# Routing of seven sequences moved into the attention ahead of the experts, with joined moves in the layers beside it

## The chip, the cores and the metric

One core of one Trainium2 chip runs the whole kernel. The metric is the time of one execution on the device in microseconds (us). Of three runs of the kernel before, the median was 2061.19 us (2058.47 to 2065.32).

## What is computed

`x` holds 8 sequences of 128 tokens with 256 columns, `ctx` a context of the same shape. Four layers follow, each a cross attention and a feed-forward network with a residual:

```
x = x + L0_xattn(ln(x), ctx, ctx);  x = x + L0_ffn(ln(x))     # 8 experts, top 2
x = x + L1_xattn(ln(x), ctx, ctx);  x = x + L1_ffn(ln(x))     # ternary weights
x = x + L2_xattn(ln(x), ctx);       x = x + L2_ffn(ln(x))     # attention, then 16 experts
x = x + L3_xattn(ln(x), ctx);       x = x + L3_ffn(ln(x))     # gated, rounded weights
```

The parts that matter here. The L1 feed-forward takes ternary weights from the mean of |w| of each matrix, and quantises rows of activations:

```
ternary(w) = round(tanh(w / (mean|w| + 1e-8))) * arctanh(mean|w|)
linear(x, w, g) = quantise(g * x * rsqrt(mean(x*x) + 1e-8)) @ ternary(w).T
L1_ffn = linear(silu(linear(x, w1, g1)) * linear(x, w2, g2), w3, g3)
```

The L2 feed-forward is a causal self attention with 16 heads of 128, then a layer of experts:

```
hid = h + attention(rmsnorm(h))
x2 = rmsnorm(hid);  probs = softmax(x2 @ gate.T)          # 16 experts
top_w, top_i = top_k(probs, 4);  top_w /= sum(top_w)
routed = sum over the 4 of top_w * w2[e](silu(w1g[e] x2) * (w1u[e] x2))
out = hid + routed + shared(x2)                           # a shared network of width 352
```

## The kernel before, in words

The stages run one after the other, each in blocks in which every engine has its own program and waits on semaphores. SyncE (SP) issues most DMAs, GpSimd (POOL) the indirect ones.

**L1 attention** (`stage_l1_xattn`, L850; from about 397 to 515 us). POOL clears `vs` (L889), builds the parity column (L905), raises the variances to the power -1/2 (L256), makes the masked keys (L913) and normalises probabilities (L921). ScalarE first copies the values into `vs` (L987), then works through 32 steps `n`, four exponentials each (L996). TensorE waits for the copies at its first step.

**L1 feed-forward** (`stage_l1_ffn`, L1058; 515.7 to 671 us). SP loads three weight matrices of 128x2048 and three gains (L1131 to L1135). VectorE normalises x (`normalise_all`, L233 and L238), waits for all loads, sums |w| of the three matrices (L1161), takes thresholds, makes the ternary weights (L1173, L1174), waits for the root mean squares, and then quantises the input of each sequence (`first`, L1187 to L1204). A step for a sequence is `gate` (L1209), `add` of the sequence before (L1234), `first` of a later pair, and `quantise_hidden` (L1215 to L1229). The last begins with the mean square `vh`, which POOL raises to a power (`rh`, L1151). In this stage VectorE also prepares some weights of the next one (L2401).

**L2 attention** (`attention_16`, L1989, causal, prefix `l2fa`; about 1178 to 1521 us). It runs 8 sequences `b` of 4 quads `i`; a quad is 4 heads. The orders are written out by hand. TensorE, for a quad: values of the quad before (L1417), side work of the even half-slot, projections of sequence b+1 (q, k, v: L2279, L2286), output projection of the quad before (L2316), side work of the odd half-slot, transposes of the probabilities (L1409), scores of the next quad (L1401). VectorE, for a quad: maximum (L1366), addition of the output (L2197), copy of the turned output (L2193), normalising the probabilities (L1374, L1376), side work of the even half-slot, copy of v (L2187), side work of the odd half-slot. ScalarE has the exponentials (L1385) and the copies. Half-slot h is 2*(4b+i) for the even and one more for the odd.

The side work of before is `GatedWeightsPrep` (L1445): it prepares the weights of the L3 feed-forward in the half-slots by a fixed table in `on_vector`. For j=0 from half-slot 11 and j=1 from 25: three mask steps (k = 0 to 2), one that inverts (k = 3), three that round (k = 4 to 6, L1542 to L1548), a diagonal (k = 7), two rows (k = 10, 11). The down weights take half-slots 40 to 48, two masks of 704 columns at 40 and 41 and two roundings at 43 and 44.

**Experts** (`moe_16`, L3003; 1522.5 to 1765 us). First comes the whole routing: mean squares on ScalarE, power on POOL (L3136), rows `x2` on VectorE (L3159), transposes, logits (L3340), softmax, comparison of every pair of the 16 scores, choice of four, count of earlier tokens of each expert (a matmul), slot and weight of every choice. POOL scatters each row to its four slots in `rows` in DRAM (32 indirect DMAs, L3148). From it comes the list of tiles (L3229 to L3249): 47 tiles of 128 rows, each with its expert's number. TensorE works on 63 units: first 16 halves of the shared network (two for each sequence), then the 47 tiles. For each unit: up (L3361), transposes of the activation (L3374, L3375), down (L3392, L3393). SP loads the expert weights (L3104 is the last of them), each tile's tokens (L3110), and stores the results.

**L3 attention** (`attention_16` not causal, prefix `l3a`, with the gated feed-forward as side work; 1765.5 to 2064 us). POOL gathers four routed rows for each token of a sequence (L2091). For sequences 0 and 1 VectorE adds them with their weights to x (L2146, four operations each), for later ones POOL does (`mix`, L2099 and on). POOL gathers sequences 0 and 1 first, then raises the variance (L2110) between other work. L1814 is one VectorE operation of the side work there.

Of the kernel before, what the change touches and what calls it, by code (L numbers as in the profile page):

```python
# [13 lines left out]
ALU = mybir.AluOpType  # L14
# [7 lines left out]
P = 128  # L22
B = 8
D = 256
KC = D // P
STAGES = range(5)
# [823 lines left out]
def stage_l1_xattn(nc, G, A):  # L850

    with ExitStack() as ctx:
# [33 lines left out]
        with nc.Block() as block:  # L886
            @block.gpsimd
            def _(pool):
                nc.gpsimd.memset(vs[:, :, :, :, :], 0.0).then_inc(zeroed, 1)  # L889
# [36 lines left out]
                keys(1)  # L926
                for n in range(N):
# [55 lines left out]
            def _(act):  # L983
                act.wait_ge(zeroed, 1)
                for s in range(2):
                    heads = lambda t: t.rearrange("p c b (g s k) -> p (c b) g s k", s=2, k=HD)[:, :, :, s, :]
                    nc.scalar.copy(heads(vs[:, s, :, :, :]), heads(G.ctxT[:, :, :, :])).then_inc(vs_made, 1)  # L987

                for n in range(N):
                    u = n % 2  # L990
                    wait(act, turned, 2 * (n - 1))
# [10 lines left out]
            def _(pe):  # L1002
# [38 lines left out]
                for n in range(N + 3):  # L1041
                    if n + 1 < N:
                        scores(n + 1)
                    if n == 0:
                        pe.wait_ge(vs_made, 2)
# [7 lines left out]
H1 = 1024  # L1053
# [4 lines left out]
def stage_l1_ffn(nc, G, A, W):  # L1058
# [5 lines left out]
    with ExitStack() as ctx:  # L1064
# [5 lines left out]
        w = [T.sb(f"w{j}", [P, NW]) for j in range(3)]  # L1070
        below = T.sb("below", [P, NW], BF16)
        tern = [T.sb(f"tern{j}", [P, NW], BF16) for j in range(3)]
        g12 = T.sb("g12", [P, 2, D])
        g3 = T.sb("g3", [P, H1])
        asum = T.sb("asum", [P, 3])
# [37 lines left out]
        order, first_order, second_order, loaded, summed, totals = (  # L1113
            T.sem("order"), T.sem("first_order"), T.sem("second_order"), T.sem("loaded"), T.sem("summed"), T.sem("totals"))
# [12 lines left out]
        with nc.Block() as block:  # L1127
            @block.sync
            def _(sp):
                for j, (name, chunks) in enumerate((("L1_w1T", KC), ("L1_w2T", KC), ("L1_w3T", HC))):  # L1130
                    sp.dma_start(w[j][:, :].rearrange("p (c o) -> p c o", c=chunks),  # L1131
                                 A[name].rearrange("(c p) o -> p c o", p=P)).then_inc(loaded, 16)
                sp.dma_start(g12[:, 0, :], row(A["L1_ffn_g1"], D)).then_inc(loaded, 16)
                sp.dma_start(g12[:, 1, :], row(A["L1_ffn_g2"], D)).then_inc(loaded, 16)
                sp.dma_start(g3[:, :], row(A["L1_ffn_g3"], H1)).then_inc(loaded, 16)  # L1135
                sp.wait_ge(loaded, 96)
                W.load(sp, A)
# [17 lines left out]
            def _(dve):  # L1155
                T.order = o = Order(dve, order)
                normalise_all(nc, G, T, xn)

                dve.wait_ge(loaded, 96)
                for j in range(3):  # L1160
                    last = nc.vector.tensor_reduce(asum[:, j:j + 1], w[j][:, :], AX.X, ALU.add,  # L1161
                                                   apply_absolute_value=True)
                last.then_inc(summed, 1)
# [8 lines left out]
                for j in range(3):  # L1172
# [4 lines left out]
                    dve.wait_ge(tern_ready, j + 1)  # L1177
                dve.wait_ge(atanh_ready, 1)
                o.step(nc.vector.tensor_scalar(atanh[:, :], atanh[:, :], 0.5, None, ALU.mult))
                dve.wait_ge(squared, 1)  # L1180
                nc.vector.tensor_scalar(vrms[:, :], ss[:, :], 1.0 / D, eps, ALU.mult, ALU.add).then_inc(ms_ready, 1)
                dve.wait_ge(rrms_ready, 1)
# [29 lines left out]
                def quantise_hidden(b, u):  # L1212
# [3 lines left out]
                        .then_inc(vh_ready, 1)  # L1216
                    dve.wait_ge(rh_ready, b + 1)
# [34 lines left out]
            def _(act):  # L1252
                act.wait_ge(T.ln_ready, 1)
# [2281 lines left out]
```

## Time and profile before

| what | value |
|---|---|
| median of three runs | 2061.19 us |
| the profiled execution | 2066.01 us |
| its span | 2064.2 us |
| TensorE (PE) busy | 1600.0 us, 78% |
| VectorE (DVE) busy | 1376.3 us, 67% |
| ScalarE (ACT) busy | 815.3 us, 39% |
| GpSimd (POOL) busy | 627.3 us, 30% |
| mean granted TensorE clock | 0.889 |

The times of stages and instructions below count from the start of the span of the profiled execution. Busy shares are means over stages with different limits, so they are to be read stage by stage. PEld is TensorE's loading of weights, which runs beside its matmuls. PEclk is the granted clock of TensorE as a share of 2.4 GHz: 1.00 is 2.4, 0.50 is 1.2 GHz. "[2.58 <-PE l2fa_psS L1401]" behind a row says that the engine had been idle for 2.58 us before it and that TensorE's work of line 1401 released it. "x4" behind a row merges four instructions that follow each other closely.

### The profile page before, as it was taken

How to read it: one execution, taken by the hardware profiler on the slowest of the kernel's cores; microseconds unless marked ns; L12 is line 12 of the kernel's file. 1: busy time of each engine (PE TensorE's matmuls, PEld its weight loads, DVE VectorE, ACT ScalarE, POOL GpSimd, SP SyncE). 2: the span in 40 equal slices, each digit the busy share in tenths (PEclk: the TensorE clock that was granted, in tenths of full speed). 3: DMA queues.
4: the chain of work that ended last, by engine and by line, in shares of the span. 5: the costliest groups of instructions: out<-in, count | busy, mean ns of one | idle time of the engine just before them, and what ended most of it. 6: DMA issues, size and time to landing. Idle time of an engine off the chain costs nothing. (4 is left out here: it accounts for less than half of the span.)

```text
span 2064.2 us, 29673 instructions
## 1 busy us (share of the span) xinstructions
PE 1600.0 (78%) x9237; PEld 1129.0 (55%) x9318; DVE 1376.3 (67%) x3775; ACT 815.3 (39%) x2357; POOL 627.3 (30%) x744
## 2 busy tenths in 40 slices
PE   3559998698144589888889589999958799498884
PEld 2424443365022366666666468888854455397872
DVE  6679969578676588887888725565347333258776
ACT  2113444355222366666667423333321122144551
POOL 0020002266200587777677430000015100533100
PEclk7579999879555799999999889999979899799996
DMA  1306520000580910000000140000043222622110
GB/s 61 107 1 174 183 81 1 1 1 1 85 151 0 342 64 1 1 1 1 1 1 1 44 151 1 15 1 1 1 167 89 72 89 89 224 103 75 65 47 11
DMA packets 104405, 129.33 MB, mean 63 GB/s; under 512 B 14208, under 2 KB 89184, under 8 KB 101056
## 3 DMA queue, kind: packets, MB, share of 16 engines
q1 hardware_dynamic: 95264, 112.39, 16.9%
q0 software_dynamic: 8992, 15.08, 3.5%
q8 instruction: 78, 1.28, 0.3%
q14 instruction: 71, 0.58, 0.1%
HBM read 85.75 MB, written 46.94 MB: 64 GB/s over the span
## 5 line engine op out<-in xcount | busy, mean ns | idle before, releaser
L580 POOL TENSOR_TENSOR l0f_diag<-g_identb,l0f_mask 128x1024 bf16<-128x1024 bf16 x16 | 32.0, 2026 | 227.7 <-PE l0f_psA L836 208.8
L2769 ACT ACTIVATE l2x_probs<-l2x_psS,l2x_nmax 128x128 f32<-128x128 f32 x256 | 91.0, 373 | 10.6 <-DVE l2x_nmax L2683 10.5
L2553 POOL TENSOR_TENSOR l2x_probs<-l2x_probs,l2x_rtotal 128x512 f32<-128x512 f32 x64 | 66.9, 1045 | 91.2 <-DVE l2x_rtotal L2689 91.2
L3129 POOL MEMSET moe_before<- 128x256 f32 x1 | 0.3, 317 | 287.2 <-POOLq L162 287.2
L3260 DVE COPY moe_xgT<-moe_psX 128x256 f32<-128x256 f32 x47 | 20.0, 425 | 99.7 <-PE moe_psX L3368 99.7
L2564 POOL TENSOR_TENSOR l2x_vsm<-l2x_vraw,l2x_smooth_row 128x512 f32<-128x512 f32 x64 | 84.7, 1344 | 3.9 <-ACT l2x_vraw L2803 3.6
L2091 POOL DMA_INDIRECT l3a_routed<-rows,slots_slot_of x32 | 31.5, 984 | 174.0 <-issue 165.8
L2914 PEld LDWEIGHTS l2x_psS<-l2x_kT,l2x_qT 128*128 128x128 f32 x512 | 66.8, 191 | 22.3 <-issue 17.9
L996 ACT ACTIVATE l1a_probs<-l1a_psS,l1a_nmax 128x256 f32<-128x256 f32 x128 | 59.0, 473 | 43.7 <-PE l1a_psT L1024 36.9
L819 PE MATMUL l0f_psH<-l0f_wT,l0f_xm 128*128 128x512 bf16 x256 | 68.0, 389 | 10.2 <-DVE l0f_h L660 9.0
L921 POOL TENSOR_TENSOR l1a_probs<-l1a_probs,l1a_rtotal 128x512 f32<-128x512 f32 x64 | 65.2, 1041 | 32.5 <-DVE l1a_rtotal L958 32.5
L3361 PE MATMUL moe_psG<-moe_w,moe_xgT 128*128 x188 | 69.2, 491 | 5.0 <-issue 1.6
L2812 ACT COPY l2x_pT<-l2x_psT 128x512 f32<-128x512 f32 x64 | 37.5, 586 | 89.6 <-PE l2x_psT L2922 89.6
L2316 PE MATMUL l3a_psY<-l3a_wo,l3a_oT 128*128 128x256 f32 x256 | 61.6, 383 | 12.4 <-DVE l3a_oT L2193 12.3
L1385 ACT ACTIVATE l2fa_probs<-l2fa_psS,l2fa_bias 128x128 f32<-128x128 f32 x128 | 45.3, 366 | 63.2 <-DVE l2fa_bias L1369 63.2
L2930 PE MATMUL l2x_psO<-l2x_pT,l2x_vsm 128*128 128x128 f32 x512 | 69.8, 281 | 0.0
L2914 PE MATMUL l2x_psS<-l2x_kT,l2x_qT 128*128 128x128 f32 x512 | 67.8, 275 | 1.8 <-ACT l2x_probs L2769 1.7
L2187 DVE COPY l2fa_v<-l2fa_psQ 128x512 f32<-128x512 f32 x32 | 22.0, 688 | 70.0 <-PE l2fa_psQ L2286 65.3
L2279 PE MATMUL l3a_psQ<-l3a_xT,l3a_wq 128*128 128x128 f32 x512 | 65.1, 282 | 2.9 <-ACT l3a_qT L2238 1.5
L2535 POOL TENSOR_TENSOR l2x_qrstd<-l2x_qve,g_minus_half 128x4 f32<-128x4 f32 x64 | 65.7, 1026 | 5.3
L3313 ACT ACTIVATE moe_gated<-moe_psG 128x176 f32<-128x176 f32 x63 | 20.0, 318 | 119.7 <-PE moe_psG L3361 111.7
L2786 ACT ACTIVATE l2x_qT<-l2x_psN,cw_head_bs,cw_head_ws 128x512 f32<-128x512 f32 x64 | 50.3, 786 | 41.4 <-PE l2x_psN L2865 41.4
(543 smaller groups left out, 4870.3 us busy)
## 6 DMA issues: line engine op xcount, KB each, us to landing
rows<-l2x_zero SPq DMA_DIRECT2D x1, 18304.0 KB, 59.9
kT_ctx<-l0f_held SPq DMA_DIRECT2D x32, 256.0 KB, 3.6
v_ctx<-l0f_held SPq DMA_DIRECT2D x32, 256.0 KB, 3.7
l3a_kT<-kT_ctx SPq DMA_DIRECT2D x8, 1024.0 KB, 6.6
l3a_v<-v_ctx SPq DMA_DIRECT2D x8, 1024.0 KB, 5.1
l0f_wrow<-in_L_ffn_w SPq DMA_DIRECT2D x24, 256.0 KB, 3.1
moe_xg<-rows SPq DMA_DIRECT2D x47, 128.0 KB, 2.0
rows<-moe_yg SPq DMA_DIRECT2D x47, 128.0 KB, 1.7
```

Of the source, the lines that this page charges most:

```text
L819: last = nc.tensor.matmul(psH[:, k, :], xm[b % 2][:, k, c, e, :], wT[:, 2 * e:2 * e + 2, c, :], start=(e == 0 and c == 0), stop=(e == E0 - ...
L921: nc.gpsimd.tensor_tensor(probs[:, u, j, :, :], probs[:, u, j, :, :], rtotal[:, u, j, :].unsqueeze(2).to_broadcast([P, 2, D]), ALU.mult)\
L996: last = nc.scalar.activation(probs[:, u, j, m, :], psS[2 * u + j][:, m, :], ACT.Exp, bias=nmax[:, u, j, m:m + 1], scale=1.0, accum_out=to ...
L2279: last = nc.tensor.matmul(psQ[bank][:, j, :], w[:, c, h * HD:(h + 1) * HD], xT[u][:, c, :], start=(c == 0), stop=(c == KC - 1))
L2316: last = nc.tensor.matmul(psY[:, :], oT[:, i % 2, j, :], wo[:, 4 * i + j, :], start=(i == 0 and j == 0), stop=(i == QUADS - 1 and j == 3))
L2535: ins = nc.gpsimd.tensor_tensor(qrstd[:, t % 2, :], qve[:, :], G.minus_half[:, 0:4], ALU.pow)
L2553: nc.gpsimd.tensor_tensor(probs[:, n % 2, :, :], probs[:, n % 2, :, :], rtotal[:, n % 2, :].unsqueeze(2).to_broadcast([P, 4, P]), ALU.mult)\
L2564: nc.gpsimd.tensor_tensor(vsm[:, j % 3, 4 * g:4 * g + 4, :].rearrange("p (g r) d -> p g r d", r=2), vraw[:, j % 2, 2 * g:2 * g + 2, :].uns ...
L2769: last = nc.scalar.activation(probs[:, n % 2, j, :], psS[:, j, :], ACT.Exp, bias=nmax[:, n % 2, j:j + 1], scale=1.0, accum_out=total[:, n ...
L2914: last = nc.tensor.matmul(psS[:, j, :], qT[:, n % 4, j, :], kT[:, n // 2 % 2, 2 * (n % 2) + j // 2, :], start=True, stop=True)
L2930: last = nc.tensor.matmul(psO[:, j, :], vsm[:, n // 2 % 3, 4 * (n % 2) + j, :], pT[:, n % 2, j, :], start=True, stop=True)
L3361: last = nc.tensor.matmul(psG[m % 3][:, 0:2 * I2], x, w, start=(c == 0), stop=(c == KC - 1))
```

## The change

**L1.** A new class `TernaryWeights` loads the three matrices and the gains during the L1 attention, and ScalarE sums |w| there, with an activation Abs over 2048 columns at steps 8, 12 and 16. The clearing of `vs` goes behind the first two groups of keys on POOL, the copies into `vs` to ScalarE's step 1, the wait of TensorE to step 3. In the L1 feed-forward the wait for the loads and the three reductions are gone; the order on VectorE is: statistics, thresholds, ternary matrix 0, normalised x, ternary matrix 1, mean squares, ternary matrix 2, first. The logarithm goes ahead of the squares on ScalarE. The add of the sequence before goes from behind the gate to behind `vh`.

```diff
+class TernaryWeights:
+    SUMS_AT = (8, 12, 16)
...
+    def sum(self, nc, act, n):
+        if n in self.SUMS_AT:
+            j = self.SUMS_AT.index(n)
+            act.wait_ge(self.loaded[j], 16)
+            wait(act, self.summed, j)
+            nc.scalar.activation(self.magnitude[:, :], self.w[j][:, :], ACT.Abs, accum_out=self.asum[:, j:j + 1])\
+                .then_inc(self.summed, 1)
...
                     nc.vector.tensor_scalar(vh[:, u:u + 1], hh[:, u:u + 1], 1.0 / H1, eps, ALU.mult, ALU.add)\
                         .then_inc(vh_ready, 1)
+                    if not is_zero(b):
+                        add(b - 1, 1 - u)
                     dve.wait_ge(rh_ready, b + 1)
...
                     gate(b, u)
-                    if not is_zero(b):
-                        add(b - 1, 1 - u)
```

**L2, routing.** A new class `Router` does the routing for one sequence at a time. Sequences 0 to 6 are routed in half-slots of the causal attention, beside `GatedWeightsPrep` (class `PrepAndRoutes`; in a half-slot the preparation comes first). For sequence s, with t = TURN_AT[s]: ScalarE's square and VectorE's variance in half-slot t-2, the rows `x2` in t-1, TensorE's transposes and VectorE's copy in t, logits, maximum and exponential in t+1, comparison in t+2, choice and TensorE's count in t+3, slots and weights in t+4. POOL has, in this order for each s: power, addition of hid to x, four scatters. All routings share one bank of PSUM with the preparation. The slots and weights of sequence 6 are made behind the last quad, its scatter and all of sequence 7 in the MoE stage.

```diff
+class Router:
+    TURN_AT = (12, 23, 28, 37, 49, 54, 60)
...
+    def compare(self, dve, s):
+        nc, o = self.nc, self.o
+        dve.wait_ge(self.exp_ready, s + 1)
+        o.step(nc.vector.reciprocal(self.total[:, :], self.total[:, :]))
+        o.step(nc.vector.tensor_scalar(self.scores, self.scores, self.total[:, :], None, ALU.mult))
+        full = [P, E2, E2]
+        other, own = self.scores.unsqueeze(1).to_broadcast(full), self.scores.unsqueeze(2).to_broadcast(full)
+        o.mark(nc.vector.tensor_tensor(self.gt, other, own, ALU.is_gt))
+        o.step(nc.vector.tensor_tensor(self.eq, other, own, ALU.is_equal))
+        o.step(nc.vector.tensor_tensor(self.eq, self.eq, self.before[:, :, :], ALU.mult))
+        o.step(nc.vector.tensor_tensor(self.gt, self.gt, self.eq, ALU.add))
+
+    def choose(self, dve, s):
+        nc, o = self.nc, self.o
+        o.step(nc.vector.tensor_reduce(self.rank, self.gt, AX.X, ALU.add))
+        o.step(nc.vector.tensor_scalar(self.chosen[:, :], self.rank, TOP2 - 0.5, None, ALU.is_lt))
+        old, new = self.earlier[:, s % 2, :], self.earlier[:, (s + 1) % 2, :]
...
+            ins = nc.vector.tensor_tensor(new, old, self.chosen[:, :], ALU.add)
+        ins.then_inc(self.chosen_ready, 1)
+        full = [P, TOP2, E2]
+        o.step(nc.vector.tensor_tensor(self.is_kth, self.rank.unsqueeze(1).to_broadcast(full),
+                                       self.numbers[:, 0:TOP2].unsqueeze(2).to_broadcast(full), ALU.is_equal))
+
+    def count(self, pe, G, s):
+        pe.wait_ge(self.chosen_ready, s + 1)
+        nc = self.nc
+        nc.tensor.matmul(self.psP, self.above[:, :], self.chosen[:, :], start=True, stop=False)
+        last = nc.tensor.matmul(self.psP, G.ones[:, :], self.earlier[:, s % 2, :], start=False, stop=True)
...
+        last.then_inc(self.counted, 1)
...
+    def on_tensor(self, pe, G, h):
+        s = self.at_slot(h, 0)
+        if s is not None:
+            self.turn(pe, G, s)
+        s = self.at_slot(h, 1)
+        if s is not None:
+            self.logits(pe, G, s)
+        s = self.at_slot(h, 3)
+        if s is not None:
+            self.count(pe, G, s)
+
+    def on_gpsimd(self, pool, G, added):
+        self.constants(pool, G)
+        for s in range(B - 1):
+            self.invert(pool, G, s)
+            self.add_hid(pool, G, s)
+            if s < B - 2:
+                self.scatter(pool, G, s)
```

**L2, experts.** `moe_16` has no routing of its own but that of sequence 7, in its units 0 to 6, and the list of tiles behind it. Ten shared halves come first (AHEAD), then the 47 tiles, then the other six halves. Behind the stores POOL gathers the rows of sequences 0 and 1 for the next stage, and VectorE mixes sequence 0 in this stage.

```diff
+        AHEAD = 2 * 5
+        tile_at = lambda m: m - AHEAD if AHEAD <= m < AHEAD + TILES else None
+        half_at = lambda m: m if m < AHEAD else m - TILES if m >= AHEAD + TILES else None
...
+                for u in range(NY):
+                    pool.wait_ge(stored[u], 16 * len(range(u, TILES, NY)))
+                R.gather(G, 0)
+                R.gather(G, 1)
```

**L3.** A class `Routed` holds the gathered rows over both stages. VectorE mixes every sequence (four operations each), ahead of its statistics; POOL only takes the powers and gathers sequence b+4 once sequence b+2 has been mixed.

```diff
-                    gather(0)
-                    gather(1)
-                    for b in range(2):
-                        pool.wait_ge(first_mixed, b + 1)
-                        gather(b + 2)
-                        invert(b)
-                    mix(2)
+                    invert(0)
+                    R.gather(G, 2)
+                    invert(1)
+                    R.gather(G, 3)
...
-                        if b + 3 < B:
-                            mix(b + 3)
+                        if b + 4 < B:
+                            pool.wait_ge(R.mixed_first, b + 3)
+                            R.gather(G, b + 4)
```

## Rows read from the trace of the kernel before

**Rows 1.** windows by stage: us, busy of PE, PEld, DVE, ACT, POOL, clock, DMA share

```profile
515.00:672.00 157.00, 51.55 (x222) 25.95 (x226) 106.56 (x228) 36.63 (x60) 17.43 (x30) 0.57 0.48 77
1210.00:1521.00 311.00, 302.34 (x2052) 260.30 (x2079) 156.05 (x332) 104.87 (x356) 6.02 (x7) 1.00 0.02 6
```

**Rows 2.** timeline, L1 attention: start, duration, engine, line, operation, [idle before <- releaser]

```profile
396.98 3.51 POOL L889 MEMSET l1a_vs<- 128x4096 f32 x1 [51.26 <-POOLq L162]
...
441.43 0.47 ACT L996 ACTIVATE l1a_probs<-l1a_psS,l1a_nmax 128x256 f32<-128x256 f32 x1 [1.81 <-PE l1a_psT L1024]
```

**Rows 3.** timeline, start of the L1 feed-forward stage

```profile
521.10 0.73 DVE L238 TENSOR_SCALAR l1f_xn<-g_x,l1f_mv,l1f_rstd 128x256 f32<-128x256 f32 x2 [1.77 <-POOL l1f_rstd L256]
...
528.81 2.29 DVE L1161 TENSOR_REDUCE l1f_asum<-l1f_w 128x1 f32<-128x2048 f32 x1 [5.04 <-DMA l1f_g<-in_L_ffn_g]
...
550.30 0.40 DVE L2401 RECIPROCAL cw_inverse<-cw_scales 128x40 f32<-128x40 f32 x1 [1.75 <-POOL l1f_rrms L1143]
550.62 0.80 DVE L1187 SCALAR_TENSOR_TENSOR l1f_y<-l1f_xn,l1f_rrms,l1f_g 128x256 f32<-128x256 f32 x2
```

**Rows 4.** timeline, one step of the L1 feed-forward stage

```profile
593.19 0.48 DVE L1234 SCALAR_TENSOR_TENSOR g_x<-l1f_psO,l1f_undo,g_x 128x256 f32 x1 [3.06 <-PE l1f_psO L1327]
...
598.03 1.28 DVE L1218 SCALAR_TENSOR_TENSOR l1f_y<-l1f_h,l1f_rh,l1f_g 128x1024 f32<-128x1024 f32 x1 [0.66 <-POOL l1f_rh L1151]
```

**Rows 5.** timeline, one quad of the L2 causal attention

```profile
1477.17 0.69 DVE L1366 TENSOR_REDUCE l2fa_nmax<-l2fa_psS 128x4 f32<-128x512 f32 x1 [2.58 <-PE l2fa_psS L1401]
...
1477.86 1.95 PE L2279 MATMUL l2fa_psQ<-l2fa_xT,l2fa_wq 128*128 128x128 f32 x16
...
1479.85 0.69 DVE L1376 TENSOR_TENSOR l2fa_probs<-l2fa_probs,l2fa_rtotal 128x512 f32<-128x512 f32 x1
...
1483.35 0.69 DVE L2187 COPY l2fa_v<-l2fa_psQ 128x512 f32<-128x512 f32 x1 [2.81 <-PE l2fa_psQ L2286]
...
1484.88 0.38 PE L1409 MATMUL l2fa_psT<-g_ident,l2fa_probs 128*128 128x128 f32 x2
...
1486.62 0.69 DVE L1366 TENSOR_REDUCE l2fa_nmax<-l2fa_psS 128x4 f32<-128x512 f32 x1 [2.58 <-PE l2fa_psS L1401]
```

**Rows 6.** timeline, a quad with a rounding step of the weights on VectorE

```profile
1373.51 0.61 DVE L1542 TENSOR_SCALAR l2fa_gw<-l2fa_gw,l2fa_winv 128x256 f32<-128x256 f32 x2
1376.53 0.69 DVE L1548 TENSOR_TENSOR l2fa_hots<-l2fa_gtotal,l2fa_up_count 128x512 bf16<-128x512 f32 x1
```

**Rows 7.** timeline, prices of the routing's kinds of work, MoE stage

```profile
1599.24 0.96 POOL L3148 DMA_INDIRECT rows<-moe_x,slots_slot_of  x1 [0.30 <-issue]
1599.66 0.41 DVE L3232 TENSOR_TENSOR moe_pairs<-moe_tiles,moe_before 1x256 f32<-1x256 f32 x1
...
1540.46 0.40 PE L3340 MATMUL moe_psX<-moe_gate,moe_x2T 128*128 128x16 f32 x1 [0.78 <-DVE moe_x2T L3164]
```

**Rows 8.** timeline, TensorE, first projection of the L3 attention

```profile
1786.33 3.75 PE L2279 MATMUL l3a_psQ<-l3a_xT,l3a_wq 128*128 128x128 f32 x16 [0.61 <-DVE l3a_xT L2175]
```

**Rows 9.** timeline, quads of the last sequence of the L2 attention

```profile
1511.98 0.69 DVE L1366 TENSOR_REDUCE l2fa_nmax<-l2fa_psS 128x4 f32<-128x512 f32 x1 [1.85 <-PE l2fa_psS L1401]
```

**Rows 10.** timeline, MoE stage: first tile, SyncE, list; and moe_w2t to landing

```profile
1615.04 0.95 PE L3361 MATMUL moe_psG<-moe_w,moe_xgT 128*128 x1 [1.56 <-issue]
...
1528.82 16.95 SPq L3104 DMA_DIRECT2D moe_w2t<-in_L2f_w2T  x1
...
1605.82 0.18 DVE L3249 CAST moe_expert_i<-moe_expert 1x47 int32<-1x47 f32 x1
...
moe_w2t<-in_L2f_w2T SPq DMA_DIRECT2D x1, 768.0 KB, 28.5
```

**Rows 11.** start of the L3 attention: VectorE's mix, and the tile l3a_wq's landings

```profile
1776.90 0.48 DVE L2146 SCALAR_TENSOR_TENSOR g_x<-l3a_routed,slots_weight_of,g_x 128x256 f32<-128x256 f32 x1 [17.40 <-DMA l3a_routed<-rows,slots_slot_of]
...
DMA to landing us min/median/max: 4.5/12.7/13.8
```

**Rows 12.** line L1814 alone, min/median/max ns: VectorE beside POOL's mix

```profile
L1814 DVE TENSOR_TENSOR l3a_up<-l3a_up,l3a_silu x8: 882/893/2334, 1861.3 to 2049.6; 128x704 f32<-128x704 f32 x8
```

More of the change, by code:

```diff
@@ L25 @@
 KC = D // P
-STAGES = range(5)
+STAGES = range(4)
 NH = 16
@@ L1177, in _ @@
                     dve.wait_ge(tern_ready, j + 1)
+                ternary(0)
+                dve.wait_ge(T.rstd_ready, 1)
+                for b in range(B):
+                    last = nc.vector.tensor_scalar(xn[:, b, :], G.x[:, b, :], T.mv[:, b, 0:1], T.rstd[:, b:b + 1],
+                                                   ALU.subtract, ALU.mult)
+                last.then_inc(T.ln_ready, 1)
+                ternary(1)
                 dve.wait_ge(atanh_ready, 1)
@@ L3123, in _ @@
                     store(i)
-                for u in range(NY):
-                    sp.wait_ge(stored[u], 16 * len(range(u, TILES, NY)))
             @block.gpsimd
             def _(pool):
-                nc.gpsimd.memset(before[:, :, :], 1.0).then_inc(made, 1)
-                nc.gpsimd.iota(numbers_i[:, :], pattern=[[1, P]], base=0, channel_multiplier=0).then_inc(made, 1)
+                routes.scatter(pool, G, B - 2)
+                routes.invert(pool, G, B - 1)
+                pool.wait_ge(routes.rrms_ready, B)
@@ L3139, in _ @@
[L3139 to L3149 removed]
+                pool.wait_ge(made, MADE)
@@ L3153, in _ @@
                 o = Order(dve, order)
-                dve.wait_ge(small_loaded, 32)
-                dve.wait_ge(squared, B)
-                nc.vector.tensor_scalar(vrms[:, :], ss[:, :], 1.0 / D, eps, ALU.mult, ALU.add).then_inc(ms_ready, 1)
-                dve.wait_ge(rrms_ready, 1)
-                for b in range(B):
-                    nc.vector.scalar_tensor_tensor(out=x2[:, b, :], in0=hid[:, b, :], scalar=rrms[:, b:b + 1],
-                                                   in1=lnw[:, :], op0=ALU.mult, op1=ALU.mult).then_inc(x2_ready, 1)
@@ L3287, in _ @@
-                for m in range(UNITS + 1):
-                    if m <= SHARED:
-                        route(m)
-                    if SHARED <= m < UNITS - 1:
-                        if m == SHARED:
-                            copy_tokens(0)
-                        copy_tokens(m + 1 - SHARED)
-                    if m > 0:
+                    s = B - 1
+                    if m == 0:
+                        routes.variance(dve, s)
+                        routes.rows(dve, G, s)
+                    elif m == 1:
+                        routes.copy_turned(dve, G, s)
+                    elif m == 2:
+                        routes.maximum(dve, s)
+                    elif m == 3:
+                        routes.compare(dve, s)
+                    elif m == 4:
+                        routes.choose(dve, s)
+                    elif m == 5:
+                        routes.assign(dve, s)
+                        list_tiles()
+                    elif m == 6:
+                        routes.weigh(dve, s)
@@ new lines, in down @@
+                    begins, ends = i is not None or n % 2 == 0, i is not None or n % 2 == 1
+                    if begins and r >= 2:
+                        last = r - 2
+                        if last < AHEAD // 2:
+                            pe.wait_ge(shared_added, last + 1)
+                        elif last < AHEAD // 2 + TILES:
+                            pe.wait_ge(yg_ready, last - AHEAD // 2 + 1)
+                        else:
+                            pe.wait_ge(shared_added, last - TILES + 1)
@@ L3404, in _ @@
+                    nc.tensor.matmul(y, actT[m % 2][0:TAIL, 1, :], tail, start=False, stop=ends).then_inc(down_done, 1)
                 for m in range(UNITS + 2):
```

667 lines of the change are left out of this document (381 added, 286 removed).

## The prediction, made before the changed kernel was run

> **What bounds the kernel now.** I read the busy time by stage first, then the timelines of the seams, then each engine's order around them. TensorE is not one bound throughout. In the L2 causal attention it is: 302 of 311 us at clock 1.00, POOL busy for 6 [rows 1]; there every wait of TensorE lengthens the kernel and other engines' free time is cheap. In the L1 feed-forward stage it is busy for 52 of 157 us and VectorE for 107 [rows 1]: VectorE's chain sets the time. Between the L2 attention (ends about 1522.5) and the first expert tile, the routing of all tokens is a chain of VectorE and POOL that covers only 16 shared halves of TensorE work.
>
> **The change part by part.** The sum is made against the profiled execution, 2066.0 us (span 2064.2), 4.8 above the median 2061.2; I subtract 4.8 at the end.
>
> *A, L1 attention.* The 3.51 us memset stands on POOL ahead of the parity chain and rstd, on which the first q and scores wait; behind the keys it is hidden [rows 2]: −3.5. The spread copies of the values (about 1.0 us each) now stand between the first two exponentials: +0.6. Three sums of |w| on ScalarE, priced at VectorE's 2.3 us for the same 2048 columns [rows 3], go into idle stretches of about 1.81 us [rows 2]; 0.4 to 0.5 of each sticks out: +1.3. The six loads go to an SP that has nothing else to issue in this stage, and the next stage's own loads start sooner for it; 0. A: **−1.6**.
>
> *B, start of the L1 feed-forward.* These leave VectorE's chain: the wait for the last load 5.04, three reductions (6.7), the totals (0.7), the wait for rstd 1.77, that for rrms 1.75 [rows 3], together 15.9; the squares finish inside the second and third ternary pass, at about 1 us of new wait. The first y, now at 550.62 [rows 3], starts **15** earlier. The Ln and the totals are covered by VectorE's normalisation statistics; uncovered they would cost 2.
>
> *C, its steps.* The add waits 3.06 for the down projection; behind vh it comes later than that result and fills the 0.66 for which VectorE waits for POOL's rh [rows 4]. Period −3.35 for five steps, −0.9 for two: **−18.6**. What is next late is the silu, ready about 0.9 before the gate needs it, so there is little more to get.
>
> *D, routing inside the L2 attention.* A quad takes 9.45 us: maximum 1477.17, q projection 1477.86, probabilities until 1480.54, v copy 1483.35, turn 1484.88, next maximum 1486.62 [rows 5]. VectorE has two gaps, 2.81 ahead of the v copy and 2.58 ahead of the maximum. An even half-slot's work fills the first, an odd one's the second. TensorE meets its even half-slot at 1477.86, the odd one at 1484.88. Prices: a VectorE operation of 256 elements 0.41; compare, with four at 128x256, 2.15; choose up to its signal 0.85; assign 0.8; weigh 1.0. One POOL scatter is 0.96+0.30, so four are 5.0 [rows 7]. A rounding step is 1373.51 to 1377.22, 3.7 [rows 6]; a mask step 1.4 (1.8 at 704 columns).
> TensorE's count waits for the choice that VectorE makes in the same half-slot. Even: the choice is done at 1480.54+0.85=1481.4, a wait of 3.6 from 1477.86. Half-slot 52 pays 3.6, 40 has a mask first (5.4), 26 a mask and VectorE 0.9 late (5.9): 14.9. Odd: half-slot 15 has a rounding first, 1484.04+3.75+0.85−1484.88, 3.8, rounded up to 4.2; 31 has roundings in 30 and 31 and a compare: 8.4. Together 12.6.
> The turn needs rows, these need POOL's power, and that stands behind four scatters, which start only when the sequence before has its slots. In half-slots 28 and 54 (one slot later) VectorE waits 5.6 inside the slot where it has 2.58, and TensorE 5.1 and 3.9: 9.0. In the other gaps of the list POOL is done in time.
> TensorE's own work (two transposes, two logit matmuls at 0.4 with their load, two counts) is 1.1 a sequence [rows 7], five times: 5.5. ScalarE's square and exponential, and POOL's hid addition, lie in idle time of their engines (POOL's 6 us of 311 grow by 28 scatters, 35 us); 0, unless the addition holds the next power, 0.6.
> The last sequence's quads have no projections to hide behind and VectorE waits 1.85 ahead of the maximum [rows 9]; three routings lie there (half-slots 56 to 63 and the end): 3.3+5.3+0.9+3.3+1.9=14.7.
> Four waits are over 5 us. [rows 8] show TensorE after a wait in the L3 stage: 3.75 for sixteen matmuls against 1.95 [rows 5], its lower level against the higher, 1.8 each: 7.2.
> D: 14.9+12.6+9.0+5.5+14.7+7.2 = **+64**. Bounds: from +37 (waits at their bare sizes, below) to +90 (a rival).
> The Trainium skill (TensorE: Matmul & The Clock Gate, HAM oscillation — how this bites in real kernels) says that idle gaps between bursts send TensorE back to half speed each time, which speaks against this change. By it all ten waits could restart slow, 18 in place of 7.2; the trace agrees in kind [rows 8], but no row here shows the clock after a wait of 3 to 4 us, so the sum keeps four.
>
> *E, MoE stage.* The first tile starts at 1615.04, 92.5 after the stage; now it waits for the later of the expert weights and the ten shared halves. The last expert weights are issued at 1528.82 and land 28.5 later [rows 10], 34.8 after the stage's start. TensorE: first shared weights about 7.5, ten halves at 2.75, the cold start, the list of tiles (1599.0 to 1606.0 [rows 7, 10], 5 of it uncovered), compare and choose 2, two more table loads on ScalarE 2: 43. So −49.5. The six halves behind the tiles cost +16.5, and the last stores and gathers run beside them, −2: **−35**. Tokens come from the scatter of sequence 7, at about 35, just ahead. Bounds −20 (list and scatter 15 later) to −42 (nothing uncovered).
>
> *F, L3.* VectorE waits 17.40 for the first gather before its first mix, and the q projection starts at 1786.33 [rows 8, 11], 20.8 into the stage. Both gathers and the first mix are now done in the stage before. It would start at 4.7, but the columns of Wq land 12.7 and 13.8 after issue [rows 11]; −12. Each later sequence puts four mixes (2.05) on VectorE, about 0.9 of which TensorE's slack takes; on the other side L1814 goes from its worst 2.33 beside POOL's mix to 0.89 [rows 12]: +1 in all. **−11**; bounds −16 and −4.
> By the Trainium skill (SBUF — State Buffer, Who interferes with whom) a VectorE operation with two SBUF inputs and a GpSimd operation that reads SBUF lock each other out. The trace agrees with the removal, 2.33 against 0.89 [rows 12]. The same page would let VectorE's work delay the scatters' descriptors; no row shows that in the attention.
>
> Sum: −1.6−15−18.6+64−35−11 = −17.2, 2048.8, less 4.8: **2044**.
>
> **Rivals.** *Waits absorbed* (for: VectorE is busy for only 156 of 311 us [rows 1], and a wait at one half-slot lets the others finish their queue before the next). Counts at their bare price 3×3.6+2×3.8=18.4, turns 2×3, own work 2.7, tail 8, no slow restarts, something above 35: D is +37, 2017. Against: the waits are dependencies within the slot, and TensorE has 3% to spare.
> *Slower than before*: each of the ten waits is followed by a second one. Mechanism: VectorE leaves the slot late by more than its 2.58 gap [rows 5], so the next maximum, exponentials and turn are late as well. Price 10×2.6=26: D is +90, 2070. It decides from about +88, where the rest (−81) is eaten up. For: half-slots 26, 31 and 28 have preparation work too. Against: elsewhere the late VectorE has two free gaps in the next quad.
> *All waits restart slow*: ten times 1.8 in place of four, D +75, 2055. For: [rows 8]. Against: no row shows the lower level after waits of 3 to 4 us. The page named above stands behind it.
> *Experts late*: the tile list or sequence 7's scatter comes later, E only −21: 2058, no change by the measure here. For: everything in it now runs in the stage where DMA already moves the expert weights.
> *The change doesn't route ahead*: excluded; seven turns stand in the list.
>
> **How the numbers follow.** Forecast (2030 to 2056) 0.46, absorbed 0.25, slower 0.17, slow restarts 0.05, experts late 0.07. About 0.3%, 6 us, is what a measurement can tell from no change, so below 2055 is faster and above 2067 slower. Faster: 0.25 and nearly all of the forecast, less its upper edge, half of slow restarts on top, and less the chance that two cases join: 0.70. Same: experts late, slow restarts in part, the forecast's edge and the slower case's lower part: 0.15. Slower: 0.15. Range 2015 to 2072, from the absorbed case to the slower one; the forecast's own range is 2030 to 2056.
>
> **What would show it.** L1 feed-forward shorter by 33, its add without a wait; attention quads of 9.45 still without routing, with TensorE idle for 3.6 to 9 where a count stands, released by the choice; turns 28 and 54 released by POOL's power behind scatters. First tile 43 after the stage's start; first L3 projection 9 after. Wrong if the attention is longer by under 45 or over 80, or if the first tile waits for the list or tokens.

## The result, and where the time went

The changed kernel took 2072.66 us (median of 20 runs), the kernel before 2063.57 us in runs beside it (20 runs): a ratio of 1.004, 95% interval 1.0024 to 1.0055. The change makes the kernel slower by about 8 us (0.4%; 5 to 11 by the interval); the forecast was 2044, 17 us faster, with a range up to 2072. The profiled execution has a span of 2073.6 us against 2064.2. Ratios here and below compare executions in the same undisturbed state; one of e6's ten took 3721.28 us and is left out of its ratio.

The windows of the changed kernel by stage (columns as in [rows 1]; L1 feed-forward, L2 causal attention, experts, L3):

```profile
516.76:639.39 122.63, 49.35 (x226) 25.59 (x226) 99.15 (x226) 36.63 (x60) 19.73 (x31) 0.63 0.53 67
1147.25:1571.16 423.91, 350.69 (x2237) 301.57 (x2237) 207.23 (x524) 116.49 (x404) 54.95 (x68) 0.89 0.11 34
1571.16:1780.18 209.02, 187.08 (x735) 108.78 (x735) 78.40 (x287) 42.25 (x117) 18.21 (x22) 0.95 0.37 117
1780.18:2073.60 293.42, 229.06 (x1632) 203.75 (x1632) 196.84 (x468) 117.04 (x366) 33.80 (x40) 0.90 0.25 87
```

Stages are cut at their first instruction in both traces, so their lengths add up to the spans (us):

| stage | before | after | difference | forecast |
|---|---|---|---|---|
| ahead of the L1 attention | 397.0 | 398.1 | +1.1 | 0 |
| L1 attention | 118.7 | 118.7 | 0.0 | −1.6 |
| L1 feed-forward | 156.5 | 122.6 | −33.9 | −33.6 |
| L2 cross attention | 505.7 | 507.9 | +2.2 | 0 |
| L2 causal attention | 344.6 | 423.9 | +79.3 | +64 |
| experts | 243.1 | 209.0 | −34.1 | −35 |
| L3 | 298.6 | 293.4 | −5.2 | −11 |
| span | 2064.2 | 2073.6 | +9.4 | −17.2 |

The L1 feed-forward and the experts came out within a microsecond of the forecast; 15 of the 26.6 us that are missing lie in the causal attention, 6 in L3. In the attention's window TensorE is busy for 351 of 424 us at a mean clock of 0.89. The waits of TensorE from the first maximum to the last projection of that stage (us in total, times, longest):

```profile
PE l2fa_psF L3148 <- DVE route_earlier L3139: 28.8, 6, 9.4
PE l2fa_psF L3096 <- DVE g_ctx L3089: 14.1, 3, 5.4
PE l2fa_psF L3148 <- DVE route_earlier L3137: 4.1, 1, 4.1
PE l2fa_psY L2320 <- DVE l2fa_oT L2197: 3.1, 4, 0.8
```

L3148 is the count, L3139 and L3137 the choice, L3096 the turn (the transposes of a sequence's rows), L3089 the rows. Seven waits for a choice and three for rows, 28.8+14.1+4.1=47.0 us, are all new. The last line is not: with the wait ahead of the very last projection, which lies outside this window, it is 3.9 us, against 4.2 before. The starts of the maxima (L1366 before, L1408 after) place them. Quads that differ by less than 1 us are left out:

| quad (half-slots) | before, us | after, us | more | what stands there |
|---|---|---|---|---|
| 7 (14, 15) | 9.79 | 14.95 | +5.2 | count of sequence 0 behind a rounding |
| 8 (16, 17) | 11.13 | 13.34 | +2.2 | the work behind that wait |
| 12 (24, 25) | 9.46 | 10.73 | +1.3 | logits, comparison |
| 13 (26, 27) | 9.45 | 23.04 | +13.6 | count of 1, assignment of 1, wait for the rows of 2 |
| 14 (28, 29) | 12.75 | 14.90 | +2.2 | turn of 2, the work behind that wait |
| 15, 16 (30 to 33) | 16.82 | 29.23 | +12.4 | count of 2 behind two roundings |
| 20, 21 (40 to 43) | 20.72 | 28.53 | +7.8 | count of 3 |
| 26, 27 (52 to 55) | 18.91 | 31.64 | +12.7 | count of 4, turn of 5 |
| 28 to 30 (56 to 61) | 15.90 | 28.60 | +12.7 | the last sequence's quads |

From the last maximum to the next stage it is 17.6 us instead of 10.5. So quads without a wait for the routing, in them or just ahead, are within 1.3 us of their length before, and each wait stands where the list TURN_AT puts it. What it drags behind it is to be seen in TensorE's own timeline of the changed kernel:

```profile
1332.31 0.19 PE L3148 MATMUL l2fa_psF<-route_chosen,route_above 128*128 128x16 bf16 x1 [5.47 <-DVE route_earlier L3139]
1332.79 3.76 PE L2283 MATMUL l2fa_psQ<-l2fa_xT,l2fa_wq 128*128 128x128 f32 x16
1336.34 2.36 PE L2283 MATMUL l2fa_psQ<-l2fa_xT,l2fa_wk 128*128 128x128 f32 x16
...
1497.45 0.18 PE L3148 MATMUL l2fa_psF<-route_chosen,route_above 128*128 128x16 bf16 x1 [3.39 <-DVE route_earlier L3139]
1497.82 3.56 PE L2283 MATMUL l2fa_psQ<-l2fa_xT,l2fa_wq 128*128 128x128 f32 x16
...
1531.27 0.18 PE L3148 MATMUL l2fa_psF<-route_chosen,route_above 128*128 128x16 bf16 x1 [2.72 <-DVE route_earlier L3139]
...
1532.67 1.91 PE L1443 MATMUL l2fa_psS<-l2fa_kT,l2fa_qT 128*128 128x128 f32 x8
...
1539.07 1.05 PE L1443 MATMUL l2fa_psS<-l2fa_kT,l2fa_qT 128*128 128x128 f32 x8
...
1559.87 0.18 PE L3148 MATMUL l2fa_psF<-route_chosen,route_above 128*128 128x16 bf16 x1 [2.72 <-DVE route_earlier L3139]
...
1560.14 0.64 PE L1451 MATMUL l2fa_psT<-g_ident,l2fa_probs 128*128 128x128 f32 x4
1561.49 1.16 PE L1459 MATMUL l2fa_psO<-l2fa_pT,l2fa_v 128*128 128x128 f32 x8 [0.72 <-issue]
1563.49 3.78 PE L2320 MATMUL l2fa_psY<-l2fa_wo,l2fa_oT 128*128 128x256 f32 x8 [0.84 <-DVE l2fa_oT L2197]
```

The sixteen matmuls of a q projection take 3.76 and 3.56 behind waits of 5.47 and 3.39, against 1.95 in [rows 5]. Behind a wait of 2.72 eight score matmuls take 1.91, against 1.05 one quad later. Behind the other wait of 2.72, the last of all, the next twelve matmuls still run at full speed (0.64 and 1.16); only behind two more short pauses, 0.72 and 0.84, does the last output projection take 3.78, against 1.99 at the same place before. These are the two levels of TensorE's clock, 1.2 and 2.4 GHz: in the 3 us behind each of the first nine waits the granted clock is 0.50 to 0.58, behind the tenth it is 0.93, and then 0.50 in the 3 us from 1562.87. The Trainium skill (TensorE: Matmul & The Clock Gate, HAM oscillation — how this bites in real kernels) describes this pattern, a burst, a wait, and a burst at half speed each time, and the trace agrees, for waits of 2.72 to 4.06 us too.

### The profile page after: what moved, and what is told of

The parts are those of the page before. It is cut to its first block and busy times, and to the rows that moved or that the text cites. A ratio compares the mean times of both kernels' runs of the same rounds, so it can differ in the third digit from the quotient of the medians.

```text
span 2073.6 us, 29963 instructions
## 1 busy us (share of the span) xinstructions
PE 1631.1 (79%) x9326; PEld 1152.2 (56%) x9326; DVE 1386.5 (67%) x3891; ACT 825.3 (40%) x2380; POOL 603.4 (29%) x738
## 5 line engine op out<-in xcount | busy, mean ns | idle before, releaser
L3066 POOL DMA_INDIRECT rows<-g_ctx,route_slot_of x32 | 32.6, 1018 | 254.6 <-DVE route_slot_of L3162 220.7
L2773 ACT ACTIVATE l2x_probs<-l2x_psS,l2x_nmax 128x128 f32<-128x128 f32 x256 | 90.9, 373 | 10.1 <-DVE l2x_nmax L2687 9.9
L3609 POOL DMA_INDIRECT routed_rows<-rows,route_slot_of x32 | 31.2, 974 | 175.0 <-DMA rows<-moe_yg 166.3
L3446 DVE COPY moe_xgT<-moe_psX 128x256 f32<-128x256 f32 x47 | 19.9, 424 | 90.8 <-PE moe_psX L3545 90.8
L2918 PEld LDWEIGHTS l2x_psS<-l2x_kT,l2x_qT 128*128 128x128 f32 x512 | 66.8, 191 | 22.3 <-issue 17.2
L2283 PE MATMUL l3a_psQ<-l3a_xT,l3a_wq 128*128 128x128 f32 x512 | 68.4, 290 | 8.2 <-DMA l3a_wq<-in_L_xattn_Wq 6.7
L2283 PE MATMUL l2fa_psQ<-l2fa_xT,l2fa_wq 128*128 128x128 f32 x512 | 74.1, 306 | 0.6 <-DVE l2fa_xT L2179 0.6
L2283 PEld LDWEIGHTS l2fa_psQ<-l2fa_xT,l2fa_wq 128*128 128x128 f32 x512 | 70.5, 220 | 2.9 <-issue 2.6
L2283 PEld LDWEIGHTS l3a_psQ<-l3a_xT,l3a_wq 128*128 128x128 f32 x512 | 64.4, 204 | 9.6 <-DMA l3a_wq<-in_L_xattn_Wq 7.3
```

Source lines behind the costliest of these rows:

```text
L2283: last = nc.tensor.matmul(psQ[bank][:, j, :], w[:, c, h * HD:(h + 1) * HD], xT[u][:, c, :], start=(c == 0), stop=(c == KC - 1))
L2773: last = nc.scalar.activation(probs[:, n % 2, j, :], psS[:, j, :], ACT.Exp, bias=nmax[:, n % 2, j:j + 1], scale=1.0, accum_out=total[:, n ...
L2918: last = nc.tensor.matmul(psS[:, j, :], qT[:, n % 4, j, :], kT[:, n // 2 % 2, 2 * (n % 2) + j // 2, :], start=True, stop=True)
```

## The experiments

Two theories were put against each other. **W**: the attention's 79 us are ten waits of TensorE, and the slow clock behind each. **V**: they are VectorE's load, which TensorE meets in one place or another.

**e1, e2, e3: the waits taken out.** e1 moves the count one half-slot later, e2 the power ahead of the scatters on POOL, e3 does both.

```diff
# e1
-        s = self.at_slot(h, 3)
+        s = self.at_slot(h, 4)
         if s is not None:
             self.count(pe, G, s)
...
     def end_tensor(self, pe, G):
         self.prep.end_tensor(pe, G)
+        self.routes.count(pe, G, B - 2)
# e2
             self.add_hid(pool, G, s)
-            if s < B - 2:
-                self.scatter(pool, G, s)
+            if s > 0:
+                self.scatter(pool, G, s - 1)
```

Expected of e1:

> TensorE's count of chosen experts goes one half-slot later (t+4), ahead of the assignment that reads it; nothing else changes. Theory W (the attention's +79 us are the ten waits of TensorE, 47.0 in the trace, and the slower clock behind each of them, about 20): the seven waits for the choice, 32.9 us, go, and with them some 12 of slow clock, so the kernel is 40 to 45 us faster than the changed kernel, about 2030. Theory V (VectorE's routing work is the load; if TensorE does not wait for the choice it waits for the next maximum or copy): at most 15 us are won, about 2058.

Measured: 2040.81 us, ratio to before 0.9875 (0.9836 to 0.9914), so 1.65% of 2065 or 34 us below the changed kernel's 1.004. TensorE's waits in e1's attention:

```profile
PE l2fa_psF L3096 <- DVE g_ctx L3089: 15.2, 3, 5.4
PE l2fa_psF L3148 <- DVE route_earlier L3139: 7.3, 2, 7.0
PE l2fa_psF L3148 <- DVE route_earlier L3137: 1.6, 1, 1.6
```

The waits for the choice went from 32.9 to 8.9 us; one stayed, 7.0 in half-slot 32, where VectorE comes late from three roundings (29 to 31) in a row. The stage went from 423.9 to 390.9. W's 40 to 45 was too much, mainly by that wait and the clock behind it; V's 15 is refuted.

Expected of e2:

> On POOL the power of the next sequence goes ahead of the scatters of the one before; nothing else changes. Theory W: the three waits of TensorE for the rows (5.4, 4.1, 4.6) vanish, with 2 us of slow clock behind each: 18 to 20 us faster than the changed kernel, about 2054. Theory V: the scatters are only moved and VectorE stays the load: under 8 us.

Measured: 2052.02 us, ratio 0.994 (0.9923 to 0.9957), 21 us below the changed kernel; the stage is 405.6. In e2:

```profile
PE l2fa_psF L3148 <- DVE route_earlier L3139: 28.8, 6, 9.4
PE l2fa_psF L3096 <- DVE g_ctx L3089: 1.5, 2, 0.8
```

The turn's waits fell from 14.1 to 1.5 and the counts' stayed at 28.8 (and 4.1) to the digit: 12.6 us of wait brought 18.3 us in the stage. The scatters, now later, kept nobody waiting.

Expected of e3:

> Both edits. Theory W: all ten waits go and the attention is 60 to 65 us shorter than in the changed kernel, 10 to 18 longer than before: about 2010. Theory V: about 2050.

Measured: 2018.85 us, ratio 0.9785 (0.975 to 0.982), 53 us below the changed kernel; the stage is 368.8, 24 above before. W said 2010 and a stage shorter by 60 to 65, V 2050; the stage is shorter by 55.1.

```profile
PE l2fa_psF L3148 <- DVE route_earlier L3139: 7.2, 2, 7.0
PE l2fa_psF L3096 <- DVE g_ctx L3089: 1.7, 3, 0.8
PE l2fa_psF L3148 <- DVE route_earlier L3137: 1.6, 1, 1.6
```

10.5 us of the 47.0 are left. 36.5 us of wait went, and 55.1 us of the stage: the other 18.6 had not been in these waits.

**e4: the waits kept, the clock held.** This separates the two parts of W.

```diff
+    FILL_TURN = {2: 18, 5: 14, 6: 15}
+    FILL_COUNT = {0: 14, 1: 19, 2: 33, 3: 18, 4: 11, 5: 9, 6: 9}
+
+    def fill(self, G, n):
+        for _ in range(n):
+            self.nc.tensor.matmul(self.spare, G.ident[:, :], G.ones[:, :], start=True, stop=True)
+
     def turn(self, pe, G, s):
+        wait(pe, self.placed, s)
+        self.fill(G, self.FILL_TURN.get(s, 0))
         pe.wait_ge(self.x2_ready, s + 1)
...
     def count(self, pe, G, s):
+        pe.wait_ge(self.exp_ready, s + 1)
+        self.fill(G, self.FILL_COUNT.get(s, 0))
         pe.wait_ge(self.chosen_ready, s + 1)
```

The numbers say how many matmuls of constants TensorE runs ahead of the count of each sequence (9 to 33) and ahead of the turns of sequences 2, 5 and 6 (18, 14 and 15).

> All ten waits stay, but TensorE first runs matmuls of constants into an unused quarter of the same PSUM bank (9 to 33 of them, about as long as each wait was; their results are read by nobody). Theory W, its clock part: the granted clock stays at 1.00 behind the waits and the kernel is 12 to 20 us faster than the changed kernel (about 2056), though the waits are as long. Rival: the slower matmuls behind the waits have another cause (late operands), the clock rows stay under 1.00 or the time stays within 5 us of the changed kernel.

Measured: 2052.37 us, ratio 0.9936 (0.9912 to 0.9959), 21 us below the changed kernel; the stage is 402.6, 21.3 shorter. First the filling matmuls and the q projections of e4's attention (busy, mean ns of one), then the q projections of the changed kernel, then the windows from the first to the last maximum, e4's first and the changed kernel's second, and last e4's q projection at the place where the changed kernel's took 3.76 (fifteen of its sixteen matmuls, merged in one row):

```profile
L3098 PE MATMUL l2fa_psF<-g_ones,g_ident 128*128 128x128 f32 x320 | 37.4, 275 | 0.0
L2283 PE MATMUL l2fa_psQ<-l2fa_xT,l2fa_wq 128*128 128x128 f32 x512 | 65.3, 282 | 0.6 <-DVE l2fa_xT L2179 0.6
```

```profile
L2283 PE MATMUL l2fa_psQ<-l2fa_xT,l2fa_wq 128*128 128x128 f32 x512 | 74.1, 306 | 0.6 <-DVE l2fa_xT L2179 0.6
```

```profile
1188.00:1532.00 344.00, 329.97 (x2353) 289.08 (x2353) 188.18 (x466) 105.56 (x371) 41.30 (x52) 1.00 0.04 14
1191.00:1553.50 362.50, 315.60 (x2044) 273.47 (x2043) 187.94 (x464) 105.64 (x371) 41.28 (x52) 0.92 0.04 14
```

```profile
1327.77 1.84 PE L2283 MATMUL l2fa_psQ<-l2fa_xT,l2fa_wq 128*128 128x128 f32 x15
```

Filling takes 37.4 us, and 11.5 are still waited (6.7, 0.9, 3.7 and 0.2), together 48.9 for the 47.0 of the changed kernel: the waits are as long. But the clock is 1.00 throughout this window where it was 0.92, and the q projections need 65.3 us instead of 74.1. So 21 of the 79 us were the slow clock, 47.0 were waiting, and the remaining 11.0 are TensorE's own work and its neighbours; that last part is what is left over, and no run isolates it (the routing's own matmuls are busy for 10.4 us in e4).

**e5: the L1 parts alone**, on the kernel before (the first diff of the change, nothing of routing, experts and L3).

> The kernel before with the L1 parts of the change alone (weights and |w| in the L1 attention, no reductions, the add behind the mean square). Theory: the L1 feed-forward stage is 34 us shorter as in the changed kernel, the L1 attention no shorter, 31 to 34 us in all, about 2031. If the L2 cross attention is again 2 us longer than before, that belongs to these parts; if it is 505.7, it belongs to the rest of the change.

Measured: 2039.10 us, ratio 0.9857 (0.9834 to 0.9879), 29.5 us faster than before (25 to 34 by the interval, 31 to 34 expected). The L1 attention is 118.7, the feed-forward 122.6, as in the changed kernel. The L2 cross attention is 505.5, so its 2.2 us belong to the rest of the change. The L3 stage, whose code is that of before, took 307.0 in this profile against 298.6, 6.6 of these 8.4 us up to its third maximum: at the start of L3, with the loads and the order of before, differences of this size can't be told from scatter by one profile each. The L1 attention scatters too: 123.8 in e1's profile, 118.7 or 118.8 in the others with that code.

**e6: POOL mixes again in L3** (sequences 2 to 7).

```diff
-                    if b >= 1:
+                    if b == 1:
                         R.mix_on_vector(dve, G, b)
...
+                    mix(2)
                     for b in range(B):
...
-                        if b + 4 < B:
-                            pool.wait_ge(R.mixed_first, b + 3)
-                            R.gather(G, b + 4)
+                        if b + 3 < B:
+                            mix(b + 3)
```

> The changed kernel, but in the L3 stage sequences 2 to 7 are mixed by POOL again (as before), 0 and 1 as in the change. My forecast priced the move of the mix to VectorE at +1 us, from 1.1 a sequence lost in quad 0 less what POOL's share of the port gave back. By the quads of both traces (+1.7 and -2.0 a sequence) the move itself is neutral: this run within 3 us of the changed kernel. Rival: the mix on VectorE is what ate the gain of the early gathers, then this run is 5 to 10 us faster.

Measured: 2074.79 us, ratio 1.0031 (1.0016 to 1.0046), the changed kernel's 1.004 within the intervals; L3 is 294.2 against 293.4. Who mixes makes no difference that these runs can tell. The line of [rows 12], in the changed kernel and in e6:

```profile
L1856 DVE TENSOR_TENSOR l3a_up<-l3a_up,l3a_silu x8: 882/891/893, 1869.3 to 2057.4; 128x704 f32<-128x704 f32 x8
```

```profile
L1856 DVE TENSOR_TENSOR l3a_up<-l3a_up,l3a_silu x8: 885/892/2336, 1868.5 to 2057.8; 128x704 f32<-128x704 f32 x8
```

The worst instance falls from 2.33 to 0.89 when POOL doesn't mix, as forecast, and the mix takes it back.

**e7: all that was found, mended together.** Beside e3: ScalarE spreads the L1 values at the start of the stage and multiplies by zero where zeros belong, so the memset is gone; SP loads all of Wq ahead of the first keys and values of L3; in half-slots 15, 16, 26, 27, 30 to 32, 40, 41, 43 and 44 VectorE does the routing ahead of the preparation.

```diff
-                nc.gpsimd.memset(vs[:, :, :, :, :], 0.0).then_inc(zeroed, 1)
...
+                for s in range(2):
+                    for other in range(2):
+                        nc.scalar.mul(heads(vs[:, s, :, :, :]), heads(G.ctxT[:, :, :, :]), float(s == other))\
+                            .then_inc(vs_made, 1)
...
-                columns(0)
-                if not causal:
-                    keys_and_values(0)
-                for i in range(1, QUADS):
+                for i in range(QUADS):
                     columns(i)
                 if not causal:
+                    keys_and_values(0)
                     keys_and_values(1)
```

> Both edits of the attention; beside them: the values of the L1 attention are spread by ScalarE at the start of the stage, zeros included, so POOL's 3.5 us memset is gone; in the L3 stage all four column blocks of Wq are loaded ahead of the first keys and values; and in eleven half-slots VectorE does the routing before the preparation of weights. Theory W: the L1 attention is 3 to 4 us shorter than in the changed kernel (VectorE's q no longer stands beside the memset), the L2 attention 5 to 7 shorter than with both edits alone (the count in half-slot 32 waits 7.0 there behind three roundings), the L3 stage 5 to 8 shorter (TensorE waits 5.0 for Wq, and runs slow after it): about 2003. If the memset did not hold VectorE up, the L1 attention stays at 118.7; if Wq is bound by the memory and not by the order, the L3 stage stays within 2.

Measured: 2006.68 us (5 runs), ratio 0.9699 (0.9683 to 0.9715), 3% faster than before and the fastest of all. The L1 attention is 115.2, 3.5 shorter. Why the memset's move had gained nothing is seen in the changed kernel (first fence) and, without the memset, in e7 (second):

```profile
404.25 6.77 DVE L984 TENSOR_SCALAR l1a_q<-g_x,l1a_mv,l1a_rstd 128x256 f32<-128x256 f32 x8 [2.60 <-POOL l1a_rstd L256]
406.08 3.51 POOL L966 MEMSET l1a_vs<- 128x4096 f32 x1
411.65 0.47 ACT L1040 ACTIVATE l1a_probs<-l1a_psS,l1a_nmax 128x256 f32<-128x256 f32 x1 [12.34 <-DVE l1a_nmax L991]
...
L984 DVE TENSOR_SCALAR l1a_q<-g_x,l1a_mv,l1a_rstd x8: 394/480/4012, 404.2 to 410.6; 128x256 f32<-128x256 f32 x8
```

```profile
401.12 3.32 DVE L983 TENSOR_SCALAR l1a_q<-g_x,l1a_mv,l1a_rstd 128x256 f32<-128x256 f32 x8 [2.53 <-POOL l1a_rstd L256]
...
405.07 0.47 ACT L1037 ACTIVATE l1a_probs<-l1a_psS,l1a_nmax 128x256 f32<-128x256 f32 x1 [4.94 <-DVE l1a_nmax L990]
```

Eight operations take 6.77 us beside the memset, one of them 4.01, and 3.32 without it; in both traces one takes 0.40 when POOL is idle and 0.56 to 0.58 beside a key. The first exponential comes 13.6 us after the stage's start in the one and 10.1 in the other. The attention went from e3's 368.8 to 365.1, the last large wait from 7.0 to 3.4: the new order within the half-slot gave 3.7, less than the 5 to 7 expected. L3 went from e3's 293.3 to 288.5, 4.8, just short of 5 to 8; its first maximum comes 19.2 after the stage's start instead of 25.2, and the other five kernels with the new L3 took 292.7 to 295.5. The L2 cross attention took 510.8, another 2.9 more, which nothing here explains.

## Why the prediction was wrong

*The step that failed* is the clock term of D: "Four waits are over 5 us ... 1.8 each: 7.2." The lower clock came behind all ten waits, the last time after two more short pauses, and it held for more than sixteen matmuls in places (after the 3.76 of the q projection in the fence above, the next sixteen took 2.36); e4 measures 21.3 us, three times the term. The term had a slip beside it: of the waits forecast in D five, not four, are over 5 us (5.9, 8.4, 5.4, 5.1 and 5.3), which would have made it 9.0. I had the rival *all waits restart slow* with its price, 18, and the page that speaks for it, and gave it 0.05, since no row before showed the clock behind a wait of 3 to 4 us. That no row shows a thing is not evidence against it: [rows 8] showed that it happens; open was only behind which waits. The rival should have stood at even odds, and the value nearer to it.

*The waits themselves* came out as worked out, one by one. Forecast 4.2, 5.9, 8.4, 5.4, 3.6 for the five counts in the body, measured 4.06, 5.47, 9.41, 5.11, 3.39; turns 5.1 and 3.9, measured 5.41 and 4.10; in the last sequence 3.3, 5.3 and 3.3, measured 2.72, 4.58, 2.72. Sum 48.4 against 47.0. That the forecast count in half-slot 15 was "rounded up" from 3.8 to 4.2 and measured 4.06 is luck. *TensorE's own work and the end* were 8.3, and 11.0 is left for them.

*A* was wrong in its mechanism: I took the memset to be hidden behind the keys, and it is on POOL; but VectorE's q is made at that very time and stood still, 4.01 us for one operation, and e7 has the 3.5 us. The other terms of A, +1.9 for copies and sums, were wrong too: from the first exponential to the end of the stage it is 105.0 us before and 105.2 after. By the Trainium skill (SBUF — State Buffer, Who interferes with whom) GpSimd and a VectorE instruction in a two-port mode, which `tensor_scalar` can enter, share a pair of ports, and whoever issues first holds it for its whole instruction; I applied this page to the mix and not to the memset. The trace agrees in kind (0.40 alone, 0.56 beside a key, 4.01 beside the memset), but no run shows which mode q ran in.

*B and C* held: first y at 19.6 after the stage's start (forecast 19.9), and the add without a wait but for the last three.

```profile
536.36 0.78 DVE L1230 SCALAR_TENSOR_TENSOR l1f_y<-l1f_xn,l1f_rrms,tw_g 128x256 f32<-128x256 f32 x2
...
L1279 DVE SCALAR_TENSOR_TENSOR g_x<-l1f_psO,l1f_undo,g_x x8: 472/475/484, 565.3 to 637.6; 128x256 f32<-128x256 f32 x4, 128x256 f32 x4
  PE l1f_psO L1369: 5.6, 3
```

5.6 us in three waits are left of 24.8 in eight (3.06 each in [rows 4]).

*E* held: first tile 44.2 after the start, forecast 43, stage −34.1 for −35. The terms that the forecast names for the 43 add up to 44.0 without the cold start, so part of the agreement on the stage is luck.

```profile
1615.35 1.45 PE L3538 MATMUL moe_psG<-moe_w,moe_xgT 128*128 x4 [1.53 <-issue]
...
PE moe_psG L3538 <- DMA moe_sht<-in_L2f_sdT: 12.1, 1, 12.1
PE moe_psT L3551 <- DVE moe_act_row L3440: 4.5, 1, 4.5
```

The 12.1 is the wait for the shared weights, counted from TensorE's last work in the attention, which nothing covers any more (I had TensorE start 7.5 after the stage's start, it was 8.2), and 4.5 is the list of tiles on VectorE ahead of an activation that TensorE needs, where I had 5.

*F* was half of its forecast. The first projection came early, and then waited:

```profile
1784.66 3.51 PE L2283 MATMUL l3a_psQ<-l3a_xT,l3a_wq 128*128 128x128 f32 x16 [1.69 <-DMA l3a_wq<-in_L_xattn_Wq]
1793.17 3.79 PE L2283 MATMUL l3a_psQ<-l3a_xT,l3a_wq 128*128 128x128 f32 x16 [5.01 <-DMA l3a_wq<-in_L_xattn_Wq]
1797.73 2.69 PE L2283 MATMUL l3a_psQ<-l3a_xT,l3a_wq 128*128 128x128 f32 x11 [0.77 <-ACT l3a_qT L2242]
```

The gathers of [rows 11] had hidden a transfer that is now the last to arrive: the second block of Wq lands 13.0 after the stage's start, as forecast, but what followed ran at the lower clock again (3.79 us for sixteen; over the stage these matmuls are busy for 68.4 us, 65.1 before), so the first maximum came 25.2 after the stage's start instead of 34.0, 8.8 for 12. Of these 8.8 us, 3.6 went again later: 1.9 by the last maximum and 1.7 behind it. That isn't the scatter of one profile, since e3 repeats it (−8.8 at the first maximum, −7.0 at the last, −5.3 for the stage); its cause is open.

*The slower rival* (a second wait behind each first) gave nearly the right time, 2070, for the wrong reason: no second long wait stands behind a first one; apart from the ten, TensorE waits 3.9 us for VectorE's copies where it waited 4.2 before. *Waits absorbed* found nothing for it: each wait is a dependency within its slot.

So: predicted −17, measured +9. The difference of 26.6 is 14 for the slow clock, 3 for TensorE's own work and the end, less 1.4 for the waits; 6 in L3, 1.6 in A, 0.9 in E, less 0.3 in B and C; 2.2 in the L2 cross attention, whose cause stays open, and 1.1 ahead of all changed code, which is scatter: that part took 393.8 to 398.1 in the nine profiles.

## What to carry to other kernels

Work put into the free slots of a stage that TensorE bounds costs little beyond its own matmuls only if TensorE doesn't wait for it: let the producer have a whole slot between its choice and the matmul that reads it, and on a queue put the short operation that the critical path needs ahead of the long ones that nobody waits for. The same routing cost 79 us with neither and 24 with both. And when a wait of TensorE is priced, the matmuls behind it are to be priced at the lower clock too, if a row anywhere in the trace shows that; filling a wait with idle matmuls is a quick way to measure how much of the loss is the clock's.

## What was not expected of the hardware

- A wait of TensorE as short as 2.72 us was followed directly by matmuls near half speed (8 in 1.91 us, 1.05 one quad later). The length alone doesn't decide: the wait ahead of the count of sequence 0 was 1.64 us in e1 and 1.63 in e3, and the 32 matmuls behind it took 2.68 and 2.98 us in e1 (granted clock 0.50 from 1271 to 1274) and 2.03 and 1.95 in e3 (1.00 in the same stretch). Filling ten waits of 47.0 us with 37.4 us of constant matmuls made the kernel 21 us faster, though they compute nothing.
- A memset of 128x4096 on POOL held up a VectorE `tensor_scalar` of 128x256 to 4.01 us instead of 0.40. Not every operation is held up: in the kernel before the same memset stood beside VectorE's eight statistics, and they took as long as in the changed kernel, where it doesn't (the row of before, then the changed kernel's). A row with one neighbour doesn't price another.

```profile
397.01 2.71 DVE L936 BATCH_NORM_STATS2 l1a_stats<-g_x 128x6 f32<-128x256 f32 x8 [0.99 <-PEq L162]
```

```profile
398.06 2.71 DVE L976 BATCH_NORM_STATS2 l1a_stats<-g_x 128x6 f32<-128x256 f32 x8 [1.00 <-PEq L162]
```

- Code that no edit touches changed by 1.6 to 5.1 us in 506 (L2 cross attention: 505.7, 505.5 in the kernels with the old later stages, 507.3 to 508.0 in those with the new ones, 510.8 in e7). What does it was not tried.
